# Keys and queries laid out by a DRAM image with duplicated parts, maxima rows by DRAM, a table for the maxima, and two blocks' q, k, v inside attention, in a chain of four layers on one core

## The reference, cut to what matters

```python
# layer 0, attention: 16 heads of 8 features
qkv = nx @ Wqkv + bqkv                       # nx: layer norm of the mixer's output
scores = einsum('bqhd,bkhd->bhqk', q, k) / sqrt(8)
scores = where(causal, scores, finfo.min)
attn = softmax(scores, axis=-1)
out = einsum('bhqk,bkhd->bqhd', attn, v).reshape(B, S, D) @ Wo + bo
```

## Time and profile before

| what | value |
|---|---|
| median of 3 runs | 1338.88 us (1336.0 to 1340.39) |
| the profiled execution, its own time | 1340.04 us |
| its span, first to last instruction | 1338.3 us |
| mean granted TensorE clock | 0.964 of full |
| busy: PE, DVE, ACT, POOL | 1172.8, 890.2, 745.3, 282.6 us |
| mixer, until attention's first scores | 0 to 246.05 us |
| attention, first exp to last copy | 247.4 to about 770 us |
| the L1134 reductions in the chain that ended last | 9% of the span |

### The profile page before, as it was taken

One profiled execution on the slowest core, in us unless ns is written; L12 is line 12 of the kernel. 1 busy time (PEld: TensorE's weight loads), 2 busy tenths in 40 slices (PEclk: granted clock), 3 DMA queues, 4 the chain that ended last, 5 costly groups with the idle time before them and its releaser, 6 DMA issues.

```text
span 1338.3 us, 15954 instructions
## 1 busy us (share of the span) xinstructions
PE 1172.8 (88%) x5776; PEld 590.3 (44%) x5776; DVE 890.2 (67%) x1676; ACT 745.3 (56%) x1100; POOL 282.6 (21%) x212
## 2 busy tenths in 40 slices
PE   4768877788999999999999999999978889779998
PEld 2444444433333333333333266655533334337776
DVE  4666765888788788887864264343439998973443
ACT  3656643444545565455678854445648667425554
POOL 3222332200000000000001120100039888840000
PEclk9779988999999999999999999999989999889999
DMA  2222267334200000000000031211113322200000
GB/s 97 62 63 64 60 112 117 85 49 91 29 1 1 1 1 1 2 1 1 1 1 26 20 109 37 95 56 40 48 63 111 118 100 84 102 1 1 8 8 17
DMA packets 52111, 62.98 MB, mean 47 GB/s; under 512 B 7864, under 2 KB 42304, under 8 KB 49984
## 3 DMA queue, kind: packets, MB, share of 16 engines
q1 hardware_dynamic: 52032, 61.95, 17.4%
HBM read 51.05 MB, written 4.46 MB: 41 GB/s over the span
## 4 chain that ended last, share of the span: by engine, by line
PE 53%; DVE 18%; POOL 8%; ACT 6%; issue 5%; DVEq 0%; POOLq 0%; ACTq 0%
DVE mx L1134 9%; PE psum L1222 8%; PE psum L1505 8%; PE psum L1192 7%; PE psum L1122 6%; POOL drive L1933 6%; PE psum L385 5%; PE psum L387 5%; PE psum L386 5%; DVE hst L1955 2%; ACT probs L1206 2%; ACT psum L1893 1%; PE psum L521 1%; PE psum L1195 1%; PE psum L1237 1%
## 5 line engine op out<-in xcount | busy, mean ns | idle before, releaser
L1206 ACT ACTIVATE probs<-psum 128x1024 f32<-128x1024 f32 (+1 forms) x320 | 288.5, 938 | 215.5 <-PE psum L1195 107.2
L1134 DVE TENSOR_REDUCE mx<-psum 128x1 f32<-128x512 f32 (+3 forms) x640 | 345.3, 602 | 63.9 <-PE psum L1122 49.6
L1122 PE MATMUL psum<-kz,qa 128*128 128x512 bf16 (+3 forms) x640 | 193.3, 354 | 36.5 <-DVE mx L1134 22.7
L1192 PE MATMUL psum<-qa,kz 128*128 128x512 bf16 (+1 forms) x640 | 184.7, 363 | 4.8 <-ACT probs L1206 2.5
L1222 PE MATMUL psum<-probs,v 128*32 128x512 f32 (+3 forms) x1280 | 149.9, 541 | 0.1
L1523 DVE TENSOR_TENSOR hid<-hid,gate_bc 128x1024 f32<-128x1024 f32 x64 | 79.0, 1242 | 106.6 <-ACT hid L1515 105.0
L1933 POOL TENSOR_TENSOR drive<-du,b_bc 128x1024 f32<-128x1024 f32 x64 | 148.7, 2359 | 1.4 <-issue 1.4
L1884 PE MATMUL psum<-hst,ident 128*128 128x512 f32 x256 | 122.8, 625 | 20.4 <-DVE u L1973 14.1
L1515 ACT ACTIVATE hid<-psum,cols 128x512 f32<-128x512 f32 x128 | 84.7, 688 | 75.6 <-PE psum L387 75.3
L1122 PEld LDWEIGHTS psum<-kz,qa 128*128 128x128 bf16 x640 | 60.9, 98 | 139.3 <-DVE mx L1134 85.9
L1955 DVE TENSOR_TENSOR_SCAN hst<-psum,hlast,drive 128x512 f32<-128x512 f32 x96 | 115.1, 1262 | 8.6 <-ACT psum L1893 5.0
(11 more groups left out here) (284 smaller groups left out, 1803.1 us busy)
## 6 DMA issues: line engine op xcount, KB each, us to landing
b_bc<-b_rows SPq DMA_DIRECT2D x16, 1024.0 KB, 4.7
cs_bc<-cs_rows SPq DMA_DIRECT2D x16, 512.0 KB, 6.5
gate_bc<-gate_rows SPq DMA_DIRECT2D x32, 256.0 KB, 3.2
ew_raw<-experts_dram SPq DMA_DIRECT2D x8, 512.0 KB, 3.6
qk_part_rows<-qk_parts SPq DMA_DIRECT2D x8, 384.0 KB, 2.6
qa<-qk_part_rows SPq DMA_DIRECT2D x48, 64.0 KB
kz<-qk_part_rows SPq DMA_DIRECT2D x96, 32.0 KB
fw_raw<-net_dram SPq DMA_DIRECT2D x11, 256.0 KB, 2.7
```

The costliest lines, as they stand in the source:

```text
L1122: ins = pe.matmul(out[:, 0:w], qa[:, b, h // 2, i * P:(i + 1) * P], kz[:, h // 8, c, h % 8, 0:w], start=True, stop=not last, skip_group_ch ...
L1134: dve.tensor_reduce(mx[:, 4 * i + h % 4, c:c + 1], fill_bank("mx", k, n)[:, 0:w], AX.X, ALU.max).then_inc(S["mx_read"], 1)
L1192: ins = pe.matmul(out[:, lo:], kz[:, h // 8, kt // TPB, h % 8, kt % TPB * P:(kt % TPB + 1) * P], qa[:, b, h // 2, lo:], start=True, stop=n ...
L1206: act.activation(probs[:, st % 2, hh, :, lo:], s_pair[n % 2][:, :, lo:], ACT.Exp, scale=SCALE).then_inc(S["p_done"], 1)
```

## The change

1. **Image with duplicates.** `part_dram` holds for each block the six groups of rows as `qa` and `kz` want them, parts repeated. `store_sp` makes 12 stores of 128 x 1 KB, each as soon as its part exists. `load_sp` makes 8 loads of 48 rows of 4 KB: four (heads 0 to 7) count on `first_loaded`, four (heads 8 to 15) on `last_loaded`. Wqkv's columns for q and k are reordered by parity on the host. `blank` is written once to DRAM (1 MB, after the third chunk's load), and `blank_sp` makes 5 loads of 4 KB pieces in place of 8 of 1 KB pieces.
2. **Maxima rows by DRAM.** `mrow_sp`: one save of 4 x 2 rows, a wait for it, two loads of 2 rows, in place of 8 transfers.
3. **Blocks 2 and 3 of q, k, v in attention items 0 to 3.** Only blocks 0 and 1 have prep in the mixer, with v one turn later than q and k. Block 2's statistics stay in turn 18, its `xn` and `inner` move to the end of turn 21; the rest is spread over items 0 and 1, and block 3's over 0 to 3. `store_sp(2)` and `load_sp(2)` stand in SP's queue between the maxima rows of items 2 and 3.
4. **A table for the maxima.** `maxima_table` weighs a step by the width of its score tiles and a unit as 0.2 + 0.8 x its width / 512, and gives each quarter of a step units in proportion, so that item k's are done 2.5 full steps or more ahead of its start. Units per step then come to 26, 10, 20, 8 in items 0 and 1; 11, 4, 10, 5 in 2 and 3; 10 to 12 in full steps and 4 or 5 in an item's last, narrow step after that; 7 in item 14's first.
5. **Mixer's end.** Six units of item 0 (before: three) in turn 16, on PE; DVE reads three of them while POOL makes the deviation of the last block's `yn`. PE enters attention when the units of items 0 and 1 are read (`mx_read`); `mrow_done` is waited for by the first products with v.
6. **Start.** x is loaded as block 0 first, the rest behind `w_raw`. POOL waits for `ln_xn` before it makes `wk`.
7. `cs_rows` is laid out by chunk, so that `cs_load_sp` reads 4 KB a partition in one piece in place of eight of 512 B.

```diff
-        def load_q_sp(sp, b):
-            sp.wait_ge(S["parts_saved"], 32 * b + 32)
-            for par in range(2):
-                for g, n in enumerate(Q_ROWS):
-                    ...
-                    sp.dma_start(qa[r0:r0 + HDA, b, :, :], src).then_inc(parts_loaded[b % 2], 16)
+        def store_sp(sp, b):
+            for n, done in enumerate(("qk_evac", "parts_mid", "parts_done")):
+                for j, rows in enumerate((Q_ROWS, K_ROWS)):
+                    sp.wait_ge(S[done], 2 * b + j + 1)
+                    for g in range(len(rows)):
+                        if rows[g] == n:
+                            sp.dma_start(part_dram[j, b, g].rearrange("e h t -> h e t"), qk_parts[:, j, n, :]
+                                         ).then_inc(S[("q_saved", "k_saved")[j]], 16)
+
+        def load_sp(sp, b):
+            sp.wait_ge(S["q_saved"], 96 * b + 96)
+            sp.wait_ge(S["k_saved"], 96 * b + 96)
...
+            for half, loaded in enumerate((first_loaded[b % 2], last_loaded)):
+                for par in range(2):
+                    rows = slice(64 * par, 64 * par + M_ROW)
+                    at = 8 * par + 4 * half
+                    sp.dma_start(qa[rows, b, 4 * half:4 * half + 4, :].rearrange("p r t -> p (r t)"),
+                                 part_dram[0, b, :, :, at:at + 4, :].rearrange("g e h t -> (g e) (h t)")).then_inc(loaded, 16)
+                    sp.dma_start(kz[rows, half, b, par, :, :].rearrange("p r t -> p (r t)"),
+                                 part_dram[1, b, :, :, at:at + 4, :].rearrange("g e h t -> (g e) (h t)")).then_inc(loaded, 16)
...
             blank_sp(sp, 2)
             mrow_sp(sp, 2)
-            sp.wait_ge(parts_loaded[0], LOADS * 16)
-            load_q_sp(sp, 2)
+            store_sp(sp, 2)
+            load_sp(sp, 2)
             mrow_sp(sp, 3)
-            load_k_sp(sp, 2)
             mrow_sp(sp, 4)
...
-        PREP_PE = {(0, 1): 1, (1, 0): 2}
-        PREP_DVE = {(0, 0): 1, (1, 0): 2}
+        PREP_PE = {(0, 0): (2, "x"), (0, 1): (2, "q"), (1, 0): (2, "k"), (1, 1): (2, "v"),
+                   (2, 0): (3, "x"), (2, 1): (3, "q"), (3, 0): (3, "k"), (3, 1): (3, "v")}
+        PREP_DVE = {(0, 1): (3, "stats"), (1, 0): (3, "apply"), (1, 1): (2, "v"), (3, 1): (3, "v")}
...
-            for hh in range(4):
-                h = 4 * grp + hh
-                for n in range(2):
-                    r = 64 * (h % 2) + M_ROW + n
-                    sp.dma_start(qa[r:r + 1, b, h // 2, :], mrow[hh:hh + 1, k % 2, n, :]).then_inc(m_loaded[k % 4], 16)
+            sp.dma_start(m_dram[k % 2].rearrange("n h t -> h n t"), mrow[:, k % 2, :, :]).then_inc(m_saved, 16)
+            sp.wait_ge(m_saved, 16 * (k + 1))
+            for par in range(2):
+                ...
...
-            pe.wait_ge(S["mrow_done"], 4)
+            pe.wait_ge(S["mx_read"], unit_base[2])
             attention_pe(pe)
...
             front_pool(o, pool, 0, 0)
+            pool.wait_ge(S["ln_xn"], 1)
             pool.wait_ge(S["in_win"], 16)
```

More of the change, by code:

```diff
@@ L810, in build, with step_cost @@
             unit_base.append(unit_base[-1] + len(units(k)))
[L812 to L821, removed]
+        def step_cost(b, kp):
+            return sum((BLK - max(0, kt - TPB * b) * P) / BLK for kt in (2 * kp, 2 * kp + 1)) / 2
@@ new lines, in unit_cost, with maxima_table @@
+        def unit_cost(k, n):
+            b, _, i, c = units(k)[n]
+            return 0.2 + 0.8 * (1 if c < b else (i + 1) / TPB)
+        STEPS = [(k, kp) for k in range(16) for kp in range(2 * (ITEMS[k][0] + 1))]
+        MX_LEAD = 2.5
+        def maxima_table():
+            starts, t = [], 0.0
+            for k, kp in STEPS:
+                starts.append(t)
+                t += step_cost(ITEMS[k][0], kp)
+            due, done, due_at = [], 0.0, 0.0
+            for k in range(2, 16):
+                done += sum(unit_cost(k, n) for n in range(len(units(k))))
+                due.append((min(max(starts[STEPS.index((k, 0))] - MX_LEAD, 0.4 * starts[STEPS.index((k, 0))]), starts[STEPS.index((14, 0))] + 1.0), done))
+            table, item, n, spent = [[[] for _ in range(4)] for _ in STEPS], 2, 0, 0.0
+            for s, (k, kp) in enumerate(STEPS):
+                for hh in range(4):
+                    dt_ = step_cost(ITEMS[k][0], kp) / 4
+                    now = starts[s] + hh * dt_
+                    left = [(d, total) for d, total in due if total > spent + 1e-6]
+                    quota = max([(total - spent) * dt_ / max(d - now, dt_) for d, total in left], default=0.0)
+                    due_at = max(due_at, spent) + quota
+                    while item < 16 and spent + unit_cost(item, n) / 2 <= due_at:
+                        table[s][hh].append((item, n))
+                        spent += unit_cost(item, n)
+                        n += 1
+                        if n == len(units(item)):
+                            item, n = item + 1, 0
+            return table
@@ L868, in prep_pool @@
                                    ALU.pow).then_inc(S["ln_rstd"], 1)
-            elif n == 1:
+            elif part == "inner":
                 if b == 0:
@@ L1121, in mx_pe @@
             last = c == b
-            ins = pe.matmul(out[:, 0:w], qa[:, b, h // 2, i * P:(i + 1) * P], kz[:, h // 8, c, h % 8, 0:w], start=True, stop=not last,
+            ins = pe.matmul(out[:, 0:w], qa[:, b, h // 2, i * P:(i + 1) * P], key_rows(h, c)[:, 0:w], start=True, stop=not last,
                             skip_group_check=True)
```

298 lines of the change are left out of this document (171 added, 127 removed).

## The result

The changed kernel takes 1335.84 us (median of 16 runs, 1332.46 to 1337.73) against 1340.39 of the kernel before in the same session (16 runs, 1335.96 to 1343.77). The ratio of the two is 0.9969, with a 95% interval of [0.9959, 0.9979]: 4.2 us faster. The forecast was 9.9 us. The direction was right, the size was not: less than half came. The profiled execution of after has a span of 1335.3 us, 3.0 less than before, at a mean clock of 0.959. An execution that ran at a much lower clock than the others of its kernel is left out of the ratios, and of e7, whose profiled execution was such a one (clock 0.880), only the first 22 us are read.

The account below looks back on a forecast made before the run. It took the mixer as a hand-over chain with no full engine and attention as mostly PE and DVE coupled through three banks; -6.5 - 8.5 + 7 - 2.5 = -10.5 us gave 1329 us, range 1314 to 1344.

Parts of the forecast that it names:

- start: Kernel's start: smaller first x transfer and `xn` unstalled by holding POOL bring the mixer's work forward, -6.5 us (-3 to -8).
- the mixer between start and end: Mixer's middle: the start's lead is carried through unchanged, and faster chunk loads gain nothing, 0 us.
- end of mixer: From the last blocks' preps to attention's first scores: removed work and waits on the chain save 8.5 us (-5 to -12).
- items 0 to 3: Attention's first block: work moved in and a new wait for item 3's rows cost +7 us (+3 to +13).
- items 4 to 14: Later attention: the table's respread units save in items 4 to 11, cost in 12 to 14, -2.5 us (-9 to +6).
- the 5.5 that I drew from that rule: Start's worth, about 5.5 us, if the first convolution operation must wait for POOL's whole 2.04 us memset.
- the detour of the maxima rows: `mrow` by DRAM: save and load in series, some 5.5 us with issues, hidden except at items 0 and 3.
- The wait for item 3's rows: At item 3's start PE stands because the rows' save queues behind block 2's loads, +3 us (0 to +8).
- the list: Work changes in items 0 to 3: block 2's moved work and item 1's `mrow`, less lighter units, together +5.1 us.
- The coupling eases: Rival, chance 0.22: an even unit mix keeps banks full and cuts a third of DVE's idle in items 4 to 13, about 1309.
- Slow loads: Rival, chance 0.14: 48-row loads run no faster than 8-row ones, PE waits for rows and blocks, 1345 us, slower.
- Saving not passed on: Rival, chance 0.22: DVE-bound attention absorbs start and end savings, item 3 waits 5, table gives 0: 1339 us, no change.

Follow-up runs that it names:

- e7: Changed kernel with POOL not held for `ln_xn`, x still in two transfers: 1337.05 us, ratio 0.9968 to the kernel before.
- e5: Changed kernel run again with no edit, as control on another chip: ratio 0.9960 to the kernel before.
- e12: e11 with block 2's stores moved ahead of item 1's maxima rows: 1335.8 us, ratio 0.9968 to the kernel before.
- e13: e1 again with no edit, on the same chip as e12: 1330.07 us, ratio 0.9924 to the kernel before.
- e1: Changed kernel with item 3's maxima rows put ahead of block 2's stores and loads in SP's queue: 1328.95 us, ratio 0.9915 to the kernel before.
- e9: Kernel before with only the change's table of units added: ratio 0.9992 to the kernel before.
- e11: e1 with block 2's q, k, v work back in the mixer, only block 3's in attention: 1346.95 us, ratio 1.0038 to the kernel before.
- e6: Kernel before with only the new start (x in two transfers, POOL held): 1333.5 us, ratio 0.9938 to the kernel before.
- e2: Changed kernel with the old spreading of maxima units and `mrow` at its old places: 1328.72 us, ratio 0.9913 to the kernel before.
- e3: Changed kernel with the old start (x in one transfer, POOL not held): 1344.6 us, ratio 1.0024 to the kernel before.
- e4: Changed kernel with v made beside q and k again in the mixer's preps: 1333.18 us, ratio 0.9942 to the kernel before.
- e8: e1 and e4 together, with table and routing two steps later, giving item 14 24 units: 1323.95 us, ratio 0.9877 to the kernel before.
- e10: Kernel before with the new start and e8's table, without image, maxima rows by DRAM or moved block 2: 1329.67 us, ratio 0.9903.

## Why the prediction was right in direction and wrong in size

The terms of the sum, against the two profiles of the changed kernel (after, and e5 in brackets):

| term | predicted | measured |
|---|---|---|
| start | -6.5 | -7.7 (-7.4) |
| the mixer between start and end (to `xn` of block 1) | 0 | +3.8 (+2.9) |
| end of mixer (to the first exp) | -8.5 | -8.5 (-8.3) |
| items 0 to 3 | +7 | +9.4 (+9.3) |
| items 4 to 14 | -2.5 | +0.2 (-1.0) |
| sum | -10.5 | -2.7 (-4.5); the span -3.0 (-4.2) |

*The start* was sized well, for a reason half wrong. x gave 3.7 for my 3.0, `xn` the 4.55, and the convolution took 0.6 back for my 1.0. But e7 shows that the first two are one edit: x alone frees `xn`, and holding POOL adds nothing. The row that I read for it had `wk` at 10.75, right after `ln_rs`, and I took that for POOL's own order; in after and e7 POOL waits for the taps until 11.15 and 10.70. The convolution's operation does stall beside POOL's memsets, 2.90 us where 0.5 is its length, as by the Trainium skill's rule ("SBUF — State Buffer", Who interferes with whom). The start gained 7.7 all the same, since only 0.6 of the stall's 2.4 us reached the scan; the 5.5 that I drew from that rule is off by 2.

*The mixer's end* came as predicted. e12 against e13 shows that 5.6 of it is the work of block 2 that left; the other edits there (six early units, the entry without `mrow`) were not run alone. PE's scores were at 234.5, not near 231, since the middle had lost 3.8. For the detour of the maxima rows I had taken a save of 2.6 us; in an idle queue its read was issued 1.4 us after it (e1).

*The middle* is the first failed step, and the largest. The prediction carried the lead of the start to the end unchanged, a term of 0, and named the clock only as a thing that could go wrong; 3.8 us were lost (2.9 in e5). Of these 3.1 lie between `xn` of block 0 and `xn` of block 1, where the same 168 matmuls ran at a lower clock. Before, then after:

```profile
157.31:194.90 37.59, 28.13 (x168) 18.45 (x168) 23.94 (x77) 18.71 (x45) 13.45 (x15) 0.86 0.50 99
```

```profile
150.28:191.01 40.73, 31.15 (x168) 20.60 (x168) 23.57 (x76) 18.70 (x45) 13.60 (x15) 0.75 0.58 130
```

In all profiles but e7's the length of this stretch goes with its own clock: 37.6 to 37.9 us at 0.86 (before, e9, e11), 38.1 and 39.0 at 0.82 (e6, e1), 39.7 and 39.9 at 0.79 (e5, e12), 40.5 to 40.9 at 0.75 (after, e2, e3, e4, e13), 41.4 at 0.71 and 0.72 (e8, e10). Neither start fixes the clock: e3, with the old one, is at 0.75, and e11, with the new one, at 0.86; e6 and e10 are one program there. So much of what after seems to lose may be chance. Whether the early start makes the low clock more likely stays open: of the eleven profiles with it (e7's left out) this stretch took 37.9 to 41.4 us, of the three without 37.6, 37.6 and 40.7. One profile gives the time of the first exp to some 7 us only (e6 against e10). Whole executions differ as much: e6's took 1328.8 to 1329.0 us at a mean clock of 0.962 to 0.964, and 1336.3 to 1337.1 at 0.955 to 0.959.

*Items 0 to 3* are the second. The wait for item 3's rows was placed rightly and priced at 3, and measured 4.0: its save was issued 5.9 us into item 2, for my 8, but its read came 7.35 us behind it. The rest measured 5.5 for the 5.1 of the list, and that is partly luck. Moving block 2 costs 1.9 (e12 against e13), where the list has 3.8 for it; the other 3.6 came with e12's other edits, and the list has 1.3 of them, `mrow` of item 1, and not the statistics of block 3. The 1 us that the lighter table was to give there wasn't to be had: 66.1 in e9 against 66.2. That range, +3 to +13, did hold it.

*The table* is the third. A weight of 1 was priced at 0.59 us in items 4 to 11: -10.5 predicted, -10.1 measured, but 1.5 of this is the clock in item 8 of before, so -8.6 at the same clock. In items 12 and 13 I took 6.5 for 12.8 of weight and 14 units; it is +8.3 at full clock (e9) and +9.6 in after. I had made them PE's alone. Item 13, +2.9 us for 5.0 of weight, fits 0.59; item 12, from 64 units to 72, takes 5.3 for 7.8, or 0.69. In its window above PE idles 5.2 us (2.4 before) and DVE 12.5, and PE's weight loads for units wait 9.8 us in it for DVE: the pair couples there as in item 10. Item 14 was not ACT's alone, as I had it: in the earlier trace rows PE is busy for 71.12 us of the last 77.5, more than ACT. It took 0.7 us for my 1.5. (The weight of items 8 to 11 before is 204.8, not 205.0, which changes nothing here.)

*The rivals.* "The coupling eases" is out: an even table is worth 1 us or nothing (e9). "Slow loads" is out: while block 2 was loaded 190 GB/s moved, and from its first issue (282.1) to the last landing (285.25 and 6.1) it took 9.3 us, for the 7 to 9 of the text. "Saving not passed on" had the wait and the idle table right, but the start passes on whole (e3, e6). The result, 1335.8, lies just outside the forecast's own range of 1322 to 1335, between the forecast and no change. That 4 us can't be told from nothing was too careful: with 16 executions of each the interval of the ratio is 1.3 us to either side. The image, the maxima rows by DRAM and `cs_rows` were not run alone, so what each is worth is not known; e10, without the three and without the moved block 2, is 3.5 us behind e8.

## What to carry to other kernels

Before a loop is made to lean on a short stage, write down what stands in the transfer queue ahead of the small transfer that the next stage waits for: one line moved here was worth about as much as the whole change (e1), and the same mistake in my own experiment cost 9 us (0.0070 between e11 and e12). Work moved between two full stages pays nothing; look for the stage that is not full, here the end of the mixer's dependency chain and the gaps of item 14. An edit that gives two savings may be one: take each alone before the second is kept. And before a few us between two profiles are put down to an edit, compare the granted clock over the same work in both.

## What the runs showed that I had not expected

- A save of 8 KB is followed by its dependent read 1.4 us after its issue in an idle queue, and 7.35 us after it behind 1.5 MB of loads from the same engine.
- 48-row loads of 192 KB take 0.42 us each to issue and land in 5.5 to 6.1 us when eight are in flight.
- One program reached its first exp at 237.4 us in one profiled execution and at 244.6 in another (e6, e10); 3.3 of these 7.2 us lie in one stretch of 40 us, at a granted clock of 0.82 and 0.72. Item 12 took 55.9 us at a clock of 1.00 and 57.3 at 0.97, in versions with the same units.
